# Edge phase of a two-layer graph network: the carried columns turned ahead of the bank clearing, the tops ahead of the first quarter of products

## What is computed

```python
h = (x @ W).reshape(n_nodes, Hh, Cc)
alpha = leaky_relu(a_src[src] + a_dst[dst])
m = jax.ops.segment_max(alpha, dst, num_segments=n_nodes)
e = jnp.exp(alpha - m[dst])
denom = jax.ops.segment_sum(e, dst, num_segments=n_nodes)
w = e / jnp.clip(denom, 1e-16)[dst]
out = jax.ops.segment_sum(w[:, :, None] * h[src], dst, num_segments=n_nodes)
```

## Time and profile before

| | |
|---|---|
| median of 3 runs | 7308.97 us (7308.75 to 7311.61) |
| the profiled execution, its own time | 7302.92 us |
| its span, first to last instruction | 7301.1 us |
| TensorE matmul busy | 5277.9 us (72%) |
| VectorE busy | 5256.5 us (72%) |
| GpSimd busy | 4947.9 us (68%) |
| ScalarE busy | 2019.5 us (28%) |
| mean granted TensorE clock | 0.81 of full speed |

### The profile page before, as it was taken

How to read it: one execution, slowest core, us unless ns; L and a number is a source line. 1 busy time by engine, 2 the same in 40 slices (tenths; PEclk the granted TensorE clock), 3 DMA queues, 4 the chain that set the end, 5 groups by cost and what they waited for, 6 DMA issues and landing times. The chain is left out here.

```text
span 7301.1 us, 109199 instructions
## 1 busy us (share of the span) xinstructions
PE 5277.9 (72%) x24127; PEld 3746.7 (51%) x24128; DVE 5256.5 (72%) x15768; ACT 2019.5 (28%) x3242; POOL 4947.9 (68%) x5343
## 2 busy tenths in 40 slices
PE   6577777777776677777777777695777777777760
PEld 5455555555555455555555555463555555555540
DVE  2677767776777777677676767897777777777779
ACT  5222222222222422222222222132222222222214
POOL 1777767777774677767676767577767777777747
PEclk8788888888888888888888888897888888888875
DMA  7444444444443544444444444364444444444434
GB/s 218 139 133 135 136 130 136 132 135 131 136 136 99 172 133 134 131 131 134 130 134 130 135 130 134 107 190 142 135 136 137 134 139 134 139 135 139 135 90 134
DMA packets 488861, 994.81 MB, mean 136 GB/s; under 512 B 147015, under 2 KB 298809, under 8 KB 488343
## 3 DMA queue, kind: packets, MB, share of 16 engines
q0 software_dynamic: 227376, 635.50, 32.4%
q1 hardware_dynamic: 190836, 292.76, 12.3%
q10 hardware_dynamic: 70514, 65.01, 2.7%
HBM read 922.29 MB, written 70.57 MB: 136 GB/s over the span
## 5 line engine op out<-in xcount | busy, mean ns | idle before, releaser
L924 POOL DMA_INDIRECT e_rows<-table,e_loaded x4704 | 4462.0, 949 | 1956.9 <-issue 1450.6
L999 PE MATMUL e_p_mm<-e_rows,e_onehot 128*128 128x264 f32 x9408 | 2579.8, 421 | 428.4 <-DVE e_rows L1118 428.4
L999 PEld LDWEIGHTS e_p_mm<-e_rows,e_onehot 128*128 128x128 f32 x9408 | 1905.2, 210 | 861.5 <-issue 512.2
L1118 DVE TENSOR_TENSOR e_rows<-e_rows,e_p_e 128x1024 f32<-128x1024 f32 x1176 | 1418.3, 1206 | 0.0
L1245 DVE SCALAR_TENSOR_TENSOR e_top<-e_mask,e_p_small,e_seg 64x128 f32<-64x128 bf16 (+1 forms) x294 | 103.2, 351 | 1427.1 <-PE e_p_small L1070 1427.1
L1110 DVE TENSOR_TENSOR e_onehot<-e_col,e_p_iota 128x512 f32<-128x512 f32 (+1 forms) x1470 | 950.8, 647 | 206.5 <-issue 192.6
L952 ACT ACTIVATE e_onehotT<-e_onehotT,minus_pidx 128x2432 bf16<-128x2432 bf16 x294 | 682.6, 2322 | 1147.3 <-DMA e_pass<-pass_rows 1147.3
L970 ACT ACTIVATE e_rows<-e_gap 128x64 f32<-128x64 f32 (+1 forms) x294 | 80.5, 274 | 2995.6 <-DVE e_gap L1276 2995.6
L984 PE MATMUL e_p_mm<-e_xmsg,e_onehot 128*128 128x264 f32 x1764 | 884.2, 674 | 0.0
L1057 PE MATMUL e_p_small<-ident,e_fwd 64*1 64x64 f32 (+1 forms) x588 | 105.1, 265 | 874.3 <-issue 862.5
L955 ACT ACTIVATE e_onehotT<-e_onehotT,one_col 128x2432 bf16<-128x2432 bf16 x294 | 682.7, 2322 | 9.5
(11 more groups left out here) (214 smaller groups left out, 5791.1 us busy)
## 6 DMA issues: line engine op xcount, KB each, us to landing
e_onehotT<-rel_rows SPq DMA_DIRECT2D x294, 608.0 KB
e_rows<-table,e_loaded POOLq DMA_INDIRECT x4704
table<-n_row ACTq DMA_DIRECT2D x196, 130.0 KB, 2.8
n_looprow<-table SPq DMA_DIRECT2D x196, 128.0 KB, 2.4
table<-n_row ACTq DMA_DIRECT2D x98, 132.0 KB, 1.7
n_node<-in_x_pad SPq DMA_DIRECT2D x98, 128.0 KB, 3.0
e_mask<-mask_rows SPq DMA_DIRECT2D x196, 64.0 KB
n_resrow<-in_x_pad SPq DMA_DIRECT2D x98, 128.0 KB, 2.5
```

The source lines that it names most:

```text
L924: pool.indirect_dma_start(rows[k][:, g, 0:TW], None, table[L], bass.IndirectOffsetOnAxis(ap=idx[k][:, g:g + 1], axis=0)).then_inc(s_gat[k] ...
L999: ins = nc.tensor.matmul(p_mm[:, bass.ds(region, MW)], onehot[:, g, :], rows[k][:, g, :], start=False, stop=True, skip_group_check=True)
L1118: return nc.vector.tensor_tensor(feats, feats, p_e[:, g4, :].unsqueeze(3).to_broadcast([P, 4, H, C]), ALU.mult)
```

## The change

TensorE's body is written in another order, and the clearing of the banks moves from `product` (g == 0) to `extras`, with another pair of waits: `erow` and `extras` where it was `erow` and `msg0`. The product with g == 0 now waits for `msg0` itself. The first quarter of products moves behind the turned tops. Nothing is added or removed; the other engines' instructions stand as they did.

```diff
-                def extras():
-
+                def extras(done):
+
+                    wait_apart(pe, st["erow"], done)
+                    wait_apart(pe, st["extras"], done)
+                    for r in range(REGIONS):
+                        nc.tensor.matmul(p_mm[:, r * BANK:r * BANK + MW], zeros[:, 0:P], zeros[:, 0:MW], start=True,
+                                         stop=False, skip_group_check=True)
                     for e in range(EXTRAS):
...
                 def product(g, k, region, done):
 
-                    if g == 0:
-
-                        wait_apart(pe, st["erow"], done)
-                        wait_apart(pe, st["msg0"], done)
-                        for r in range(REGIONS):
-                            nc.tensor.matmul(p_mm[:, r * BANK:r * BANK + MW], zeros[:, 0:P], zeros[:, 0:MW], start=True,
-                                             stop=False, skip_group_check=True)
-                        extras()
-                    elif g % 4 == 0:
+                    if g % 4 == 0:
                         pe.wait_ge(st[f"msg{g // 4}"], done)
...
                     last.then_inc(st["lookup"], 1)
-                    products(0)
                     wait_apart(pe, st["carry"], now)
                     for o, src in ((256, outf), (257, outb)):
                         last = nc.tensor.matmul(p_small[0:HG, o:o + 1], flat(src), ones_row[0:1, 0:1],
                                                 start=True, stop=True)
                     last.then_inc(st["colsum"], 1)
-                    products(1)
+                    if not first:
+                        extras(past)
                     wait_apart(pe, st["top"], now)
                     nc.tensor.transpose(p_top[:, 0:HG], top[:], ident[0:HG, 0:HG]).then_inc(st["topT"], 1)
+                    products(0)
+                    products(1)
                     products(2)
...
+                extras(W0 + WINDOWS)
                 for g in range(G):
                     product(g, (WINDOWS - 1) % BUFS, regions[g], W0 + WINDOWS)
```

## The result

The changed kernel takes **6936.76 us**, median of 4 runs (6934.54 to 6939.61), against 7308.9 us for the kernel before (7308.75 to 7311.61): ratio 0.949, 95% interval 0.9474 to 0.9507. The gain is 372 us where 287 were forecast. The profiled execution took 6934.54 us, its span is 6932.6 us.

What follows compares the result with a forecast made beforehand. TensorE and VectorE waiting for each other was taken as the bound. Windows of 21.28, 21.58 and 21.63 us falling to 20.5 give 2.99 us by 96 windows, 287 us: 7022 us forecast, range 6945 to 7135 us.

Steps and rivals of the forecast that it cites:

- What bound the kernel: TensorE and VectorE wait for each other in every window, with GpSimd just behind at 20.1 to 20.4 us.
- Both waits of the loop: TensorE's products wait 428.4 us for VectorE's messages; VectorE waits 1427.1 us for carried columns turned by TensorE.
- Columns, VectorE, tops: Earlier columns cost 0 (at most 25 us); VectorE proceeds earlier, tops precede quarter 0; message waits of 1.46 us a window go.
- criterion of 0.2 us a window: Sign against the step on order: a wait for the carry before the carried columns above 0.2 us a window.
- GpSimd: Gathers start 0.8 us later at no cost, but no window gets shorter than GpSimd's 20.1 to 20.4 us.
- The 1.86 us gap: Gap between GpSimd's gathers in about one window in six, adding up to 0.26 us to its mean window.
- wanted near 41 us: Gathers end 34.4 us behind a window's turn and are wanted near 41 us, so their later start costs nothing.
- The clock: Falls of TensorE's clock settle the window at 20.5 us instead of 19.9, giving back about 0.4 of 1.46 us.
- GpSimd becomes the bound: Rival: TensorE's clock stays up and all 358.3 us of GpSimd's waits are collected; 6951 us, chance 0.10.
- The long low stretch: Second rival: 10.2 us clock lows in two windows of three add 1.0 us, windows 20.9 us; 7133 us, chance 0.14.
- TensorE waits for the carry: Slower rival: carry 2.0 us later than read, TensorE stands 1.8 us a window; 7400 us, chance 0.03.

Runs made afterwards that it cites:

- e15: The kernel before the change with only 4 of 16 gathers started in a window, other tiles keeping older rows: 7341.93 us.
- e16: The changed kernel with only 4 of 16 gathers started in a window, other tiles keeping older rows: 6882.28 us.
- e17: The changed kernel with clearing and extra products put ahead of the carried columns, then quarter 0 and tops, and 4 of 16 gathers: 6800.82 us.
- e5: The kernel before the change with 14 of 16 gathers: 9577.29 against 10212.34 us, ratio 0.9379.

## Why the prediction was right or wrong

**What bound the kernel** was right. Both waits of the loop are gone, and e15 against e16 gives their removal 460 us once GpSimd is out of the way. TensorE's busy time hardly moved, as forecast.

**Columns, VectorE, tops**: right in the order of events. The carry was forecast 0.22 us early in one window, and is 0.20 early in the one shown, but that holds for the phases with 4 heads only. With 8 heads TensorE waits for it in 96 windows, 60.3 us of the 66.7 in the whole span, 0.6 a window:

```profile
PE e_p_small L1066 <- DVE e_outb L1235: 60.3, 96, 1.5
```

0 was taken, with 25 us as the upper bound: the length of one scan was too small a measure for what 8 heads add on the way to the carry, and the criterion of 0.2 us a window is passed. It did no harm that shows: by e17, with a quarter of the gathers, a window of the third phase is 20.5 us long with a wait for the carry or without. VectorE stands 3.8 us in front of the scans, forecast 3 to 5.

**GpSimd**: the price was right in kind, too high at its upper end. The 1.86 us gap was added to make 20.4. It isn't part of the gathers' pace: in the first two phases it is gone, and the floor is 20.1. That the gathers land well before they are wanted ("wanted near 41 us") was wrong: where every window is as short as GpSimd's floor, no lead builds up. ScalarE waits for the last gather from the start of each phase on, 2.1 us in the third window of the first phase and 1.2 us in the fourth, and in nearly every window after.

**The clock** is the step that failed: "If the falls keep it, each comes 0.6 us later in its window than the last one did [...] until it is 20.5 us long. I take that as where it settles". The third phase came to that number, 20.51 us at 20.5 between falls; whether by this mechanism is not shown. In the first two phases the falls also come 17 us apart, which the three distances read before (20.5 and 23.9) didn't show; 20.5 was no smallest distance. What the runs showed in its place: without GpSimd the windows there are 19.34 us long (e16), and GpSimd's 20.1 us for 16 gathers decides (20.09 and 20.11 measured). The forecast was (20.5 - 20.1) x 2 x 98 = 78 us too high by this, which with the 6 us that 96 instead of 98 windows make is nearly the whole miss of 85 us.

**The rivals.** "GpSimd becomes the bound" (0.10; 6951 us) was right in two phases out of three and nearest in its number, but for a reason that was wrong: the clock was to stay up, and it fell to 0.756. The long low stretch did become common, two windows in three and more, as the second rival said. Yet the windows are not 20.9 us. Its price of 1.0 us can't be right on top of 19.9: e16 has lows of 6.9, 10.2 and 10.2 us and windows of 19.34. No run takes that price apart, so it stays open. "TensorE waits for the carry" came true in the third phase with 0.6 us a window, far from the 1.8 at which the kernel would be slower.

## What to carry to other kernels

When two engines wait for each other in every turn of a loop, look for the one small instruction that each wants from the other and put it ahead of the bulk; what it brings is about the sum of the waits, until the engine just behind sets the pace. Work out that engine's floor from its bare pace, without gaps that the loop itself may cause, and compare it in every phase. An engine that is ahead of the others while the window is longer than its own pace has no such lead once the window is as short as that pace. And a distance between falls of the clock, read from a few windows, is no law for a shorter window: an experiment with most of the suspected engine's work left out shows the own length of the others at once.

## What was not expected of the hardware

- TensorE's clock and the window settle together. Over four orders of the same work and three phases with a quarter of the gathers, the settled windows are 19.34, 20.48 or 21.62 us in all cases but e15's first two phases (21.05, 21.21), with falls 17.1, 20.5 and 23.9 us apart whose mean distance is the window. A gain between two of them can vanish: in the third phase e16 waits 1.14 us for the carry in each window and e17 doesn't, but its pause before the row ends is 0.75 us longer, and the windows are as long.
- The same kernel takes 7309 us in the first comparison, 7314 us on one chip of the experiments and 10210 to 10260 us on five others. On the latter VectorE's next instruction came 11.3 us late while GpSimd's gathers follow one another. Two gathers fewer give 2.2 us a window (e5), and with a quarter of them the kernel before takes 7341.93 us there. What differs between the chips is open.
- A lower mean clock (0.756, was 0.81) went with a faster kernel, and with a quarter of the gathers 0.757 and 0.784 went with the same windows.
